# Expert rows added to their tokens' rows in DRAM inside the expert loop, in place of a gather behind it

## What is computed

```python
logits = xt @ router_w.T + router_b
probs = jax.nn.softmax(logits, axis=-1)
topk_p, topk_i = lax.top_k(probs, TOP_K)
onehot = jax.nn.one_hot(topk_i, N_EXPERTS, dtype=probs.dtype)
gates = jnp.sum(onehot * topk_p[..., None], axis=1)

def expert_step(acc, packed):
    w1e, b1e, w2e, b2e, ge = packed
    h = jax.nn.gelu(xt @ w1e.T + b1e, approximate=False)
    y = h @ w2e.T + b2e
    return (acc + y * ge[:, None], None)
...
x = x + _L0_ffn_ref(_layernorm(x, axis=-1)[None], ...)[0]
```

## Time and profile before

| | us |
|---|---|
| median of three runs | 794.92 |
| the profiled execution | 788.58 |
| its span, first to last instruction | 786.4 |
| PE busy (matmuls) | 713.9 (91%) |
| VectorE busy | 432.8 (55%) |
| ACT busy | 221.6 (28%) |
| GpSimd busy | 126.3 (16%) |
| DMA | 109.28 MB, 139 GB/s over the span |

### The profile page before, as it was taken

One profiled execution on the slowest core, in us unless ns is written; L12 is line 12 of the kernel. 1 busy time (PEld: TensorE's weight loads), 2 busy tenths in 40 slices (PEclk: granted clock), 3 DMA queues, 4 the chain that ended last, 5 costly groups with the idle time before them and its releaser, 6 DMA issues.

```text
span 786.4 us, 11874 instructions
## 1 busy us (share of the span) xinstructions
PE 713.9 (91%) x3591; PEld 433.7 (55%) x3592; DVE 432.8 (55%) x1360; ACT 221.6 (28%) x456; POOL 126.3 (16%) x191
## 2 busy tenths in 40 slices
PE   4888899999999999999999999999996299999935
PEld 2544455455555555555554457768784276677601
DVE  5548763378778778787744443353445323333337
ACT  2313211223223233233232033232352044334300
POOL 6054440000000000000004100020202210000054
PEclk9999999999999999999999999999998599999965
DMA  9600000064260716455277700011217595333367
GB/s 296 177 0 1 1 0 2 36 233 175 108 254 30 283 38 231 152 186 190 94 281 275 311 0 1 0 41 41 81 45 277 213 382 200 129 129 116 122 192 237
DMA packets 48881, 109.28 MB, mean 139 GB/s; under 512 B 6842, under 2 KB 6858, under 8 KB 46384
## 3 DMA queue, kind: packets, MB, share of 16 engines
q1 hardware_dynamic: 43616, 85.82, 30.2%
q0 software_dynamic: 4912, 20.60, 7.4%
q10 hardware_dynamic: 288, 2.10, 0.7%
HBM read 47.35 MB, written 61.16 MB: 138 GB/s over the span
## 4 chain that ended last, share of the span: by engine, by line
PE 81%; issue 5%; POOL 4%; DVE 3%; DMA 3%; ACT 1%; SPq 0%; POOLq 0%; ACTq 0%; DVEq 0%
PE bank L1227 12%; PE bank L1210 10%; PE bank L1318 8%; PE bank L1374 7%; PE bank L1109 7%; PE bank L1178 7%; PE bank L1146 7%; PE bank L1387 6%; PE bank L1264 6%; PE bank L1189 4%; PE bank L1249 4%; POOL arena L614 2%; PE bank L1345 2%; DMA arena<-in_wqkv 2%; DVE arena L860 1%
## 5 line engine op out<-in xcount | busy, mean ns | idle before, releaser
L860 DVE TENSOR_SCALAR arena<-iota,arena 125x128 f16<-125x128 f16 x392 | 113.2, 289 | 44.0 <-PE bank L1109 32.7
L862 DVE TENSOR_SCALAR arena<-iota,arena 125x320 f16<-125x320 f16 x392 | 120.1, 306 | 0.0
L688 ACT ACTIVATE arena<-bank 128x416 f32<-128x416 f32 (+1 forms) x120 | 62.3, 519 | 155.1 <-PE bank L1210 152.1
L892 DVE TENSOR_SCALAR arena<-bank 128x416 f32<-128x416 f32 (+1 forms) x120 | 69.1, 591 | 61.8 <-PE bank L1210 61.7
L1227 PE MATMUL bank<-arena 128*64 128x416 f32 (+1 forms) x480 | 97.2, 525 | 0.4 <-DVE arena L892 0.4
L1109 PE MATMUL bank<-arena 125*128 125x320 f16 x392 | 71.8, 301 | 8.7 <-DVE arena L862 8.5
L1178 PE MATMUL bank<-arena 128*128 128x416 f32 (+1 forms) x192 | 74.7, 538 | 2.4 <-ACT arena L629 1.4
L1318 PE MATMUL bank<-arena 128*128 128x384 f32 (+2 forms) x256 | 70.3, 430 | 0.0
L1374 PEld LDWEIGHTS bank<-arena 128*128 128x128 f32 x448 | 52.9, 197 | 20.9 <-issue 20.9
L1374 PE MATMUL bank<-arena 128*128 128x128 f32 x448 | 55.1, 283 | 10.1 <-issue 10.1
L1049 DVE COPY arena<-arena 128x1024 f32 x30 | 20.8, 694 | 75.6 <-issue 68.0
(11 more groups left out here) (213 smaller groups left out, 994.8 us busy)
## 6 DMA issues: line engine op xcount, KB each, us to landing
slots<-arena SPq DMA_DIRECT2D x6, 5376.0 KB, 17.1
slots<-arena SPq DMA_DIRECT2D x2, 5120.0 KB, 16.2
arena<-in_ew POOLq DMA_DIRECT2D x9, 1024.0 KB, 7.0
arena<-slots SPq DMA_DIRECT2D x32, 256.0 KB, 2.8
slots<-arena SPq DMA_DIRECT2D x28, 256.0 KB, 2.1
arena<-in_ew SPq DMA_DIRECT2D x5, 1024.0 KB, 20.2
arena<-in_x SPq DMA_DIRECT2D x8, 512.0 KB, 6.1
arena<-in_gw SPq DMA_DIRECT2D x2, 2048.0 KB, 15.6
```

The source lines that it names most:

```text
L688: act.activation(probs[0:kt, s % NPB, 0, 0:n], bank[2 * (s % 2)][0:kt, 0:n], ACT.Relu).then_inc(p0_ready, 1)
L860: dve.tensor_scalar(ring[:, at_slot:at_slot + P], iota16[0:CE, 0:P], window_cols[:, i % WBUF, 1, k:k + 1], None, ALU.is_equal)
L862: dve.tensor_scalar(ring[:, at_slot + P:at_slot + OHW], iota16[0:CE, :], window_cols[:, i % WBUF, 0, k:k + 1], None, ALU.is_equal).then_in ...
L892: dve.tensor_single_scalar(probs[0:kt, s % NPB, 1, 0:n], bank[2 * (s % 2) + 1][0:kt, 0:n], 0.0, op=ALU.max).then_inc(p1_ready, 1)
```

## The change

**In the loop** DVE no longer copies an expert tile but multiplies it by the rows' gates. GpSimd then adds the tile's 128 rows to the tokens' rows in a new DRAM tensor `sums`, by one indirect DMA with an add. It waits until this has landed before it issues the next, since two tiles can hold the same token. SP's stores of the tiles go. GpSimd also fetches, at the head of a loop turn, for each of the two tiles a *note*: for each row the token's number and its gate.

**Notes.** They are made by 20 more indirect DMAs of 8 bytes a row, which put (token, gate) at the place in `notes` that answers to the row's slot. `notes` is first filled with numbers past the last token and gates of zero, so that unused rows add nothing to a row that matters. All notes are loaded to SBUF once ahead of the loop.

**Moved work.** SP stores the tokens' rows to `sums` as they get ready. The experts' loads and the counting of landed experts go from GpSimd to SP. The loads of `xg` in the loop go from SP to ACT, behind ACT's copies. **Behind the loop** SP loads `sums` back to `xr` in 10 DMAs, DVE adds the bias part (now from four banks in turn), and SP stores. The 20 gathers and the 20 scaled adds go.

```diff
     xs = nc.dram_tensor("slots", [XS_ROWS, D], f32, kind="Internal").ap()
+    sums = nc.dram_tensor("sums", [N + P, D], f32, kind="Internal").ap()
+    notes = nc.dram_tensor("notes", [P * XS_TILES, 2], f32, kind="Internal").ap()
...
@@ -404,9 +417,24 @@
             for e in (0, EXP - 1):
                 expert(e)
 
+            def store_x2(t):
+                sp.wait_ge(x2_ready, t + 1)
+                sp.dma_start(sums[t * P:t * P + rows(t), :], xr[0:rows(t), t, :]).then_inc(x2_stored, 16)
+
+            for t in range(6):
+                store_x2(t)
             sp.wait_ge(hid_ps, KH * len(FC_TILES))
             for e in (9, 10, 11):
                 expert(e)
+            for t in range(6, NT):
+                store_x2(t)
+
+            def count_expert(e):
+                sp.wait_ge(ew_in[e], 16)
+                sp.sem_inc(w_ready, 1)
+
+            for e in range(3):
+                count_expert(e)
 
             sp.wait_ge(route_ready, 1)
...
@@ -416,17 +444,18 @@
                 sp.wait_ge(xgt_ps[a], 1)
                 sp.dma_start(xg[:, a, :], rows_of(2 + a)).then_inc(xg_in[a], 16)
 
-            n = sp.value_load(npair[0:1, 0:1], min_val=1, max_val=(MAXT - 3) // 2)
-            with sp.Fori(0, n) as j:
-                for a in range(2):
-
-                    sp.wait_ge(xgt_ps[a], j + 2)
-                    sp.dma_start(xg[:, a, :], rows_of(2 * j + 4 + a)).then_inc(xg_in[a], 16)
-                for a in range(2):
-                    sp.wait_ge(y_saved[a], j + 2)
-                    sp.dma_start(rows_of(2 * j + a), y_sb[:, a, :]).then_inc(y_stored[a], 16)
-            for a in range(2):
-                sp.wait_ge(xg_in[a], 16 * (n + 2))
+            sp.wait_ge(xg_in[1], 16)
+            late = [3, 4, 5, 6, 7, 8, 12, 13, 14]
+            expert(late.pop(0))
+            expert(late.pop(0))
+            for e in range(3, EXP):
+                count_expert(e)
+                if late:
+                    expert(late.pop(0))
+
+            sp.wait_ge(sums_done, 1)
+            for t in range(NT):
+                sp.dma_start(xr[0:rows(t), t, :], sums[t * P:t * P + rows(t), :]).then_inc(sums_in[t // 2], 16)
...
             pool.wait_ge(zero_filled, 16 * HEADS)
-            for t in range(NT):
-                pool.wait_ge(slots_ready, 1 + sum(1 for tiles in FC_TILES if tiles[-1] < t))
-                for k in range(2):
+            notes_v = notes.rearrange("(p t) c -> p t c", p=P)
+            ramp(clear_notes.bitcast(i32)[:, :, 0], [[0, XS_TILES]], N, 1)
+            link(pool.memset(clear_notes[:, :, 1], 0.0))
+            pool.dma_start(notes_v, clear_notes[:, :, :]).then_inc(notes_cleared, 16)
+            pool.wait_ge(notes_cleared, 16)
+            for f, tiles in enumerate(FC_TILES):
+                pool.wait_ge(slots_ready, f + 1)
+                for t in tiles:
+                    for k in range(2):
+                        pool.indirect_dma_start(
+                            out=xs, out_offset=bass.IndirectOffsetOnAxis(ap=slot[0:rows(t), k, t:t + 1], axis=0),
+                            in_=x2n[0:rows(t), t, :], in_offset=None).then_inc(scattered, 16)
+                pool.wait_ge(gates_ready, f + 1)
+                for t in tiles:
+                    for k in range(2):
+                        pool.indirect_dma_start(
+                            out=notes, out_offset=bass.IndirectOffsetOnAxis(ap=note_at[0:rows(t), k, t:t + 1], axis=0),
+                            in_=note[0:rows(t), t, k, :], in_offset=None).then_inc(noted, 16)
+            pool.wait_ge(noted, 16 * 2 * NT)
+            pool.dma_start(all_notes[:, :, :], notes_v).then_inc(notes_in, 16)
+
+            pool.wait_ge(tiles_ready, 1)
+            n = pool.value_load(npair[0:1, 0:1], min_val=1, max_val=(MAXT - 3) // 2)
+            pool.wait_ge(x2_stored, 16 * NT)
+            pool.wait_ge(notes_in, 16)
+            with pool.Fori(0, n) as j:
+                for a in range(2):
+                    i = pool.value_load(tile_at[0:1, bass.ds(2 * j + a, 1)], min_val=0, max_val=XS_TILES - 1)
+                    pool.tensor_copy(note_now[:, a, :].unsqueeze(1), all_notes[:, bass.ds(i, 1), :]).then_inc(note_ready[a], 1)
+                for a in range(2):
+                    pool.wait_ge(note_ready[a], j + 1)
+                    pool.sem_inc(may_add, 1)
+                    pool.wait_ge(y_saved[a], j + 2)
+                    pool.sem_inc(may_add, 1)
                     pool.indirect_dma_start(
-                        out=xs, out_offset=bass.IndirectOffsetOnAxis(ap=slot[0:rows(t), k, t:t + 1], axis=0),
-                        in_=x2n[0:rows(t), t, :], in_offset=None).then_inc(scattered, 16)
-
-            pool.wait_ge(xg_in[1], 16)
-            pool.wait_ge(mix_ps, NT)
-            late = [3, 4, 5, 6, 7, 8, 12, 13, 14]
-
-            def load_next():
-                e = late.pop(0)
-                pool.dma_start(arena[:, expert_at(e):expert_at(e) + EW], ew[e]).then_inc(ew_in[e], 16)
-
-            load_next()
-            load_next()
-            for e in range(EXP):
-                pool.wait_ge(ew_in[e], 16)
-                pool.sem_inc(w_ready, 1)
-                if e >= 3 and late:
-                    load_next()
-
-            pool.wait_ge(route_ready, 1)
-            n = pool.value_load(npair[0:1, 0:1], min_val=1, max_val=(MAXT - 3) // 2)
-            for a in range(2):
-                pool.wait_ge(y_stored[a], 16 * n + 16)
-                pool.sem_inc(rows_stored, 1)
-            pool.wait_ge(rows_stored, 2)
-            for t in range(NT):
-                for k in range(2):
-                    pool.indirect_dma_start(
-                        out=yg[0:rows(t), k, t, :], out_offset=None, in_=xs,
-                        in_offset=bass.IndirectOffsetOnAxis(ap=slot[0:rows(t), k, t:t + 1], axis=0)
-                    ).then_inc(yg_in[t], 16)
+                        out=sums, out_offset=bass.IndirectOffsetOnAxis(ap=note_now.bitcast(i32)[:, a, 0:1], axis=0),
+                        in_=y_sb[:, a, :], in_offset=None, compute_op=ALU.add).then_inc(y_stored[a], 16)
+                    pool.wait_ge(y_stored[a], 16 * j + 16)
+                    pool.sem_inc(y_free[a], 1)
+            pool.sem_inc(sums_done, 1)
...
@@ -754,6 +790,11 @@
                     act.wait_ge(xgt_ps[a], j + 2)
                     act.activation(xg_t[:, a, :, :], bank[4 + a][:, :].rearrange("p (k n) -> p k n", k=KD),
                                    copy).then_inc(xgt_saved[a], 1)
+                    lies = act.value_load(tbase[0:1, bass.ds(2 * j + 4 + a, 1)], min_val=0, max_val=XS_ROWS - P)
+                    act.dma_start(xg[:, a, :], xs[bass.ds(lies, P), :]).then_inc(xg_in[a], 16)
...
                 link(dve.reciprocal(red3[:, tt], red2[:, tt]))
                 link(dve.tensor_tensor(pr, pr, over_e(red3[:, tt], n), ALU.mult))
-                dve.tensor_reduce(gate[:, 0, tt], pr, X, ALU.max)
+                dve.tensor_reduce(note[:, tt, 0, 1], pr, X, ALU.max)
+                dve.tensor_single_scalar(note_lo[:, :, tt], slot[:, :, tt], P - 1, op=ALU.bitwise_and)
+                dve.tensor_single_scalar(note_at[:, :, tt], slot[:, :, tt], 7, op=ALU.arith_shift_right)
                 link(dve.tensor_tensor(tmp[:, tt, :], pr, oh2[:, tt, :], ALU.mult))
-                dve.tensor_reduce(gate[:, 1, tt], tmp[:, tt, :], X, ALU.add)
+                dve.tensor_reduce(note[:, tt, 1, 1], tmp[:, tt, :], X, ALU.add)
+                dve.scalar_tensor_tensor(out=note_at[:, :, tt], in0=note_lo[:, :, tt], scalar=float(XS_TILES),
+                                         in1=note_at[:, :, tt], op0=ALU.mult, op1=ALU.add)
                 mask_v = mask16[:, tiles[0] * EXP:(tiles[-1] + 1) * EXP].rearrange("p (t e) -> p t e", e=EXP)
                 link(dve.tensor_tensor(gates[:, tt, :], pr, mask_v, ALU.mult))
                 dve.sem_inc(gates_ready, 1)
...
+            dve.tensor_single_scalar(tile_at[:, :], tbase[:, :], 7, op=ALU.arith_shift_right).then_inc(tiles_ready, 1)
...
@@ -1057,19 +1104,18 @@
                     take_w1(a, 2 * j + 2 + a)
                 for a in range(2):
                     dve.wait_ge(y_ps[a], j + 1)
-                    dve.wait_ge(y_stored[a], 16 * j + 16)
-                    dve.tensor_copy(y_sb[:, a, :], bank[6 + a][:, :]).then_inc(y_saved[a], 1)
+                    dve.wait_ge(y_free[a], j + 1)
+                    dve.wait_ge(note_ready[a], j + 1)
+                    dve.tensor_scalar(y_sb[:, a, :], bank[6 + a][:, :], note_now[:, a, 1:2], None,
+                                      ALU.mult).then_inc(y_saved[a], 1)
 
             for t in range(NT):
                 r = rows(t)
+                dve.wait_ge(sums_in[t // 2], 32)
                 dve.wait_ge(gb_ps, t + 1)
-                link(dve.tensor_tensor(xr[0:r, t, :], xr[0:r, t, :], bank[2 + t % 2][0:r, :], ALU.add))
+                link(dve.tensor_tensor(xr[0:r, t, :], xr[0:r, t, :], bank[t % 4][0:r, :], ALU.add))
```

(41 more changed lines are left out.)

## The result

The changed kernel takes 858.46 us (median of four runs, 856.12 to 859.99) against 794.76 for the kernel before on the same chips: 1.080 times as long, with a 95% interval of 1.077 to 1.083. The profiled execution has a span of 854.4 us, against 786.4.

What follows compares the result with a forecast made beforehand. GpSimd's queue was to bound the loop at 11.6 us a turn: 653.5 + 13 x 11.6 + 15 = 819.3 us of span, against 786.4, or 828 us in the median. The range was 784 to 872.

Steps and rivals of the forecast that it cites:

- A: In the loop, the time from an add's start to its landing: 4.4 us, from 3.1 to 5.9.
- Two adds, each with 0.3 us ahead of it: In GpSimd's loop turn, two adds, each started 0.3 us after what precedes it and waited for until landed.
- The notes: In GpSimd's loop turn, two note copies take 2.04 us plus about 0.1 for the branch; DVE's scaling adds nothing.
- The first turn: Its adds run beside the experts' loads, 5.5 us more on landing; first lands at 645.8, second at about 653.5.
- The tail: Behind the loop, loads and stores of 2.56 MB each, 13.3 us, plus a 2.1 us landing: about 15 us.
- What was to cost nothing: Notes' scatters, DVE's small operations, SP's stores to sums, ACT's added loads, earlier expert counting: 0 us, at most 4 gained.
- That cover: Before the loop, GpSimd is ready near 633, ahead of the first tile at 635.5: a thin 2.5 us.
- the earlier count of experts: Before the first two copies, DVE's 7.6 us wait for landed experts goes, but PE's first product starts no sooner: 0 counted.
- Rival 1: In the loop, adds land in 2.6 us or less, PE stays the bound; 784 us in the median, chance 0.17.
- Rival 2: In the loop, PE idles and its clock halves, 16.2 us of work a turn; some 888 us, chance 0.07.
- VectorE's copies against GpSimd's descriptors: In the loop, weight copies beside the first add may delay it 0.4 us; by the skill, 0.7 to 1.4 a turn.

Runs made afterwards that it cites:

- six banks: The changed kernel with the bias products behind the loop in six PSUM banks in turn, not four; 854.48 us, 1.077 of the kernel before.
- no add: The changed kernel with the loop's 28 indirect DMAs overwriting rows in place of adding, so the sums are left out; 815.33 us in a single run.
- notes ahead: The changed kernel with each tile's note fetched while the other tile's add is under way, still one tensor; 841.82 us, 1.060 of the kernel before.
- both edits: The changed kernel with a second sums tensor for each pair's second tile, and each note fetched once its buffer's add landed; 805.50 us, 1.013 of the kernel before.

## Why the prediction was right, and what was mis-sized

The direction and the mechanism held. GpSimd's queue became the bound of the loop, PE's work fits inside its turn, the tail got shorter, and 858.5 lies in the range of 784 to 872. The size, +33 us, was about half of the measured +64. That the range still holds the result is in part luck: its upper part was drawn for an A of up to 5.9. With the measured A of 4.8 the prediction's own sum gives 839, and the other 19 us come from terms for which it had no range. In the span the forecast was 819.3 and the result 854.4; the 35 us are these:

| term | forecast | measured | difference |
|---|---|---|---|
| start of the first add | 635.9 | 638.4 | 2.5 |
| first pair, to its second landing | 17.6 | 20.6 | 3.0 |
| 13 turns | 150.8 | 176.7 | 25.9 |
| tail from the last landing | 15 | 18.7 | 3.7 |

- **"A = 3.1 + 0.64 + 0.7 = 4.4 us."** Measured 4.8. Of the 2 us by which a turn was too short, 0.8 come from here. The build-up came this close by luck: the least, 3.1, was too high (a scatter alone lands in 2.7), and what the add puts on it was priced too low, at 1.3 where it is 2.1. Of these, GpSimd's issue of 1.55 us, 0.6 over a scatter's, had no term.
- **"Two adds, each with 0.3 us ahead of it."** This is the step that was furthest off. The 0.3 us was read between DMAs that follow one another without a wait. Behind a wait for a semaphore it is 0.78 and 0.98 us: 1.1 us a turn, 14 in all.
- **The notes.** Forecast 2.1 us a turn with the scaling hidden. Measured 2.2 (1.17 and 1.03), but the scaling is not hidden: GpSimd issues the first add when the first tile is scaled, and the second note lies beside it. The sum is right, its parts are not. With the notes and the scaling off the path, the gaps fell by 1.65 us and the turn by 1.16.
- **The first turn.** Adds of 9.9 and 9.6 us; the first was forecast at 9.9, the second at 7.4, because the stretch of the experts' loads was taken to end at 650; the last of them landed at 660.9 (and at 654.4 in the kernel before).
- **The tail.** 18.7 against 15; with two more banks 17.8. The forecast counted bytes and one landing, and had the bias products done and VectorE's additions keeping up at 0.68 us each. They start 1.0 us apart, the last four wait for PE up to 1.0 us each, and in the version with six banks they are the longest part of what is left.
- **What was to cost nothing.** GpSimd had the first notes at 628.9 and then waited 9.5 us for VectorE. That cover was not thin. PE's first product again stood behind 4.0 us of "issue", as in the earlier trace rows, so the earlier count of experts gained nothing, as forecast. The 2.5 us at the start are most likely no part of the change: SP's load of the graph weights already stands at 427.63 against 425.28 in the kernel before, ahead of anything that the change touches except one small ramp, and in the four kernels that are alike up to there (changed, no add, notes ahead, six banks) the first add starts anywhere from 638.4 to 641.2.
- **Rival 1** (adds land fast, PE stays the bound): the adds do not, at 4.8. Landing fast would not have been enough either, and here the prediction was wrong without the result showing it. Beside its two landings a turn holds 3.97 us and not 2.8, so A would have to be 2.3 for a turn of 8.54. The kernel without the add, whose landings are 2.7 and 3.9, has a turn of 10.68 and takes 815, more than the kernel before. PE is the bound again (8.53 us a turn) only where a scatter waits for no other either. The Trainium skill's fit ("DMA: Bandwidth & Descriptors", Anatomy of one DMA) gave an estimated 2.6 us: that agrees with the lone scatter's 2.73 and is 2.2 short of the add.
- **Rival 2** (PE's clock falls): it fell, to 0.88 over the loop, and cost nothing, since the second products at the lower level (6.3 us) still end before GpSimd's turn. From 660 to 740 us it was 0.88 in the version with a turn of 12.4 us too, 0.96 in the one with 10.7, and 1.00 in those with 9.8 and 10.5.
- **VectorE's copies against GpSimd's descriptors.** In the changed kernel a copy overlaps the first issue of a turn by 0.3 us only (772.01 to 772.34), and the issue took 1.55 us, against 1.54 for the one without a copy beside it; the copy paid, with 0.82 in place of 0.69. In the version with both edits, where the copies fall on the issues, the issues took 1.89 and 1.63 us, and the second copy 0.97. So it is 0.1 us a turn here and some 0.4 there, not the 0.7 to 1.4 of the prediction's estimate. That estimate rests on the Trainium skill ("SBUF — State Buffer", SBUF: two separate sides), by which the one that comes second is blocked for the whole of the other; the traces agree that the two hold each other up, but not for the whole of the copy: at 705.50 a copy of 0.70 us lies inside an issue that is 0.34 us longer than one alone.

## What to carry to other kernels

A chain in which one DMA waits for the landing of the one before is priced by the whole loop from landing to landing: the landing, the engine's path from semaphore to issue (here 0.8 to 1.3 us, not the 0.3 between DMAs issued back to back), and whatever its queue does in between. Compare that with the turn of the engine that bounds the loop, before counting what the tail gives back. Where two writers can be given places of their own, the wait and the read of an accumulating DMA both go; here that turned 8% lost into about 1% gained (0.993 and 0.989 of the kernel before).

## What the runs showed of the hardware

- A scatter of 128 rows of 2 KB lands 2.7 us after its start when alone, and in 3.2 to 4.4 beside two plain loads of 256 KB. With an add it lands in 4.8 us almost alone (changed kernel), in 4.7 to 6.2 beside two such loads (notes ahead), in 5.4 to 5.5 where two adds are issued one behind the other, and in 9.6 to 9.9 beside 1 MB loads.
- An add takes GpSimd 1.55 us to issue, an overwriting scatter 0.96. From a landing to the start of the next add, with nothing but semaphore and register instructions on the way, GpSimd takes 0.97 us, and 1.34 across the end of its loop.
- PE's granted clock was 0.88 in a loop where PE waited 3 to 4 us in each turn of 13.6, 0.96 in one of 10.7 us a turn, and 1.00 in loops of 9.8 and 10.5.
